# Turning x by DMA transposes of its half words in place of TensorE, in FFN pairs 1 and 3 and attention's first two blocks

## The reference

```
x = x + 0.5 * FFN(layernorm(x))
x = x + attention(layernorm(x))      # one head of 128, two sequences of 1024 rows
x = x + 0.5 * FFN(layernorm(x))
FFN(y) = (silu(y @ Wg) * (y @ Wu)) @ Wd     # Wg, Wu 512 x 1376, Wd 1376 x 512, 4-bit packed
```

## Time and profile before

| | us |
|---|---|
| median of 3 runs | 831.31 (831.05 to 831.92) |
| span of the profiled execution, first to last instruction | 829.4 |
| TensorE busy in it | 814.2 |
| VectorE, ScalarE, GpSimd busy | 494.9, 273.1, 252.1 |

### The profile page before, as it was taken

One profiled execution on the slowest core, in us unless ns is written; L12 is line 12 of the kernel. 1 busy time (PEld: TensorE's weight loads), 2 busy tenths in 40 slices (PEclk: granted clock), 3 DMA queues, 4 the chain that ended last, 5 costly groups with the idle time before them and its releaser, 6 DMA issues.

```text
span 829.4 us, 10560 instructions
## 1 busy us (share of the span) xinstructions
PE 814.2 (98%) x3932; PEld 670.7 (81%) x3932; DVE 494.9 (60%) x809; ACT 273.1 (33%) x471; POOL 252.1 (30%) x203
## 2 busy tenths in 40 slices
PE   4999999999999999999999999999999999999998
PEld 4777778878888888788898888888878888888786
DVE  7989945766554544547766896545346644443452
ACT  3433433555111121333656871111123311211221
POOL 5656614652115061303064371062401110110100
PEclk9999999999999999999999999999999999999999
DMA  6899958865854532234053159544454155344121
GB/s 164 275 331 295 326 185 298 342 243 210 287 181 140 175 130 71 105 108 152 1 178 128 40 183 379 198 154 151 127 166 142 49 194 175 128 154 150 30 102 51
DMA packets 73405, 143.04 MB, mean 172 GB/s; under 512 B 26092, under 2 KB 37028, under 8 KB 68362
## 3 DMA queue, kind: packets, MB, share of 16 engines
q1 hardware_dynamic: 66676, 130.97, 46.0%
q10 hardware_dynamic: 5814, 7.17, 2.5%
q0 software_dynamic: 864, 4.23, 1.9%
HBM read 104.30 MB, written 37.98 MB: 172 GB/s over the span
## 4 chain that ended last, share of the span: by engine, by line
PE 94%; POOL 1%; DVE 1%; DMA 1%; ACT 1%; issue 1%; ACTq 0%; SPq 0%; DVEq 0%; POOLq 0%
PE ps L813 53%; PE ps L806 37%; PE ps L824 2%; PE ps L1198 2%; DMA tab_rest<-sc_part 1%; POOL blk L2214 1%; PE ps L892 0%; ACTq L1538 0%; POOL xres L2324 0%; DMA zq_gu<-in_L_ffn_up_qzeros 0%; DVE stats L1718 0%; POOL xres L2329 0%; ACT xT L1315 0%; PE ps L1123 0%; POOL rstd L2219 0%
## 5 line engine op out<-in xcount | busy, mean ns | idle before, releaser
L806 PE MATMUL ps<-blk,ring 128*128 128x512 f32 (+1 forms) x1386 | 320.9, 389 | 0.5 <-POOL blk L2214 0.5
L806 PEld LDWEIGHTS ps<-blk,ring 128*128 128x128 f32 (+1 forms) x1386 | 256.7, 185 | 58.5 <-POOL blk L2214 1.0
L813 PE MATMUL ps<-wd,hT 128*128 128x512 f32 (+1 forms) x1056 | 251.6, 391 | 0.1
L813 PEld LDWEIGHTS ps<-wd,hT 128*128 128x128 f32 (+1 forms) x1056 | 197.0, 188 | 42.2 <-DVE h L1877 0.5
L2266 POOL TENSOR_TENSOR h<-h,u 128x512 f32<-128x512 f32 (+1 forms) x33 | 42.8, 1297 | 321.3 <-ACT h L1446 321.3
L813 PE MATMUL ps<-xT,wp 128*128 128x512 f32 x480 | 112.6, 390 | 0.3 <-issue 0.3
L813 PEld LDWEIGHTS ps<-xT,wp 128*128 128x128 f32 x480 | 89.8, 188 | 19.6 <-POOL wp L2214 0.6
L1710 DVE TENSOR_TENSOR u<-ps,p1s 128x512 f32<-128x512 f32 (+1 forms) x66 | 45.4, 688 | 95.8 <-PE ps L806 95.8
L1446 ACT ACTIVATE h<-h 128x512 f32<-128x512 f32 (+1 forms) x33 | 20.9, 632 | 177.4 <-DVE h L1710 177.4
L1710 DVE TENSOR_TENSOR h<-ps,p1s 128x512 f32<-128x512 f32 (+1 forms) x33 | 22.8, 691 | 63.9 <-PE ps L806 63.9
L1710 DVE TENSOR_TENSOR u<-ps,u 128x512 f32<-128x512 f32 (+1 forms) x66 | 45.6, 691 | 24.6 <-PE ps L806 23.5
(11 more groups left out here) (130 smaller groups left out, 894.5 us busy)
## 6 DMA issues: line engine op xcount, KB each, us to landing
ring<-wsaved SPq DMA_DIRECT2D x29, 1024.0 KB, 5.1
ring<-wsaved SPq DMA_DIRECT2D x33, 768.0 KB, 4.3
wsaved<-wp SPq DMA_DIRECT2D x10, 1024.0 KB, 5.0
stream<-xres SPq DMA_DIRECT2D x32, 256.0 KB, 2.4
xn<-stream SPq DMA_DIRECT2D x8, 1024.0 KB, 8.1
xres<-stream SPq DMA_DIRECT2D x32, 256.0 KB, 4.0
wfull<-wf ACTq DMA_DIRECT2D x20, 256.0 KB
wsaved<-wp SPq DMA_DIRECT2D x10, 512.0 KB, 5.5
```

What stands on the lines that cost most here:

```text
L806: mm = pe.matmul(ps[0:w, bank, :], ring[:, slot, which, a, kt, 0:w], blk[:, which, b, kt, :], start=not onto and kt == 0 and n == 0, stop= ...
L813: mm = pe.matmul(bank_ap, lhs(a), rhs(b), start=first and n == 0, stop=last and n == 2)
```

## The change

The three pieces of TensorE work in `bottom` are gone (96 transposes: blocks 2, 3, 4, 5, 10, 11). In their place, for each of these blocks: ScalarE copies each normalised tile of 128 rows into two planes of 16-bit words, the low and the high halves of its float32 values (`to_planes`, four copies of 128 x 1024 words a block, each waiting for the one before, since a tile's planes are written over the tile before it); SP stores the planes to DRAM (four DMAs of 256 KB) and issues one DMA transpose that reads the 1024 x 512 words of 16 bit and writes them turned into `xn`, where pairs of words form float32 values again. ScalarE and VectorE then read the turned tiles from SBUF, not from PSUM; the copy `x21` of A21 falls away in pairs 1 and 3.

```diff
+PLANED = (2, 3, 4, 5, 10, 11)
+        planes_early = place("planes_early", [P, 2, HID], U16, xres_at)
+        planes_late = place("planes_late", [P, 2, HID], U16, t13_at)
...
+            def store_planes(t):
+                for r in range(RT):
+                    sp.wait_ge(s_planes, planes_made(t, r))
+                    sp.dma_start(planes[t][r * P:(r + 1) * P, :, :], plane_rows(t, r)).then_inc(d_planes[t % 2], 16)
+
+            def turn_planes(t):
+
+                sp.wait_ge(*planes_stored(t))
+                sp.dma_start_transpose(xn[:, t % 2, :, :].bitcast(U16), planes[t].rearrange("n h c -> (n h) c")).then_inc(d_xT[t % 2], 16)
...
             store_rows(0, stream, 0)
-            load_residual(1, x, ROWS)
             for j in range(1, NT):
                 if j + 2 < NT:
                     load_full(j + 2)
                 save_t(j)
+                if j == 6:
+                    store_planes(2)
+                if j == 7:
+                    turn_planes(2)
+            store_planes(3)
 
             sp.wait_ge(s_up, 2 * NT)
             for i in (NT - 4, NT - 3, NT - 2, NT - 1):
                 sp.wait_ge(d_kept[i], ALL_KEPT)
             load_block(0)
+            turn_planes(3)
+            load_residual(1, x, ROWS)
             load_block(1)
...
                 load_block(n + 2)
+                if n in (6, 8):
+                    store_planes(4 if n == 6 else 5)
+                if n == 7:
+                    turn_planes(4)
+            turn_planes(5)
...
+                    if n in (NT + 6, NT + 9):
+                        store_planes(10 if n == NT + 6 else 11)
+                    if n in (NT + 7, NT + 10):
+                        turn_planes(10 if n == NT + 7 else 11)
...
-                    if i == first:
-
-                        pe.wait_ge(s_sum, 2 * RT * q + RT)
-                        if q == 1:
-                            pe.wait_ge(s_ln[4], RT)
-                            turn(4, range(KT))
-                        else:
-                            turn_pair(q + 1, 0)
-                    if i == second:
-                        if q == 1:
-                            pe.wait_ge(s_ln[5], RT)
-                            pe.wait_ge(s_alo, KT)
-                            turn(5, range(KT))
-                        else:
-                            turn_pair(q + 1, 1)
...
+            def to_planes(t, tiles=range(RT)):
+
+                for r in tiles:
+                    if r == 0:
+
+                        if t == 2:
+                            act.wait_ge(d_st[0], 16)
+                        elif t != 4:
+                            act.wait_ge(*planes_stored(PLANED[PLANED.index(t) - 1]))
+                    else:
+
+                        act.wait_ge(s_planes, planes_made(t, r - 1))
+                    act.wait_ge(s_ln[t], r + 1)
+                    copy(plane_rows(t, r), xn[:, t % 2, r, :].bitcast(U16).rearrange("p (c h) -> p h c", h=2)).then_inc(s_planes, 1)
...
                     if i in (5, 6, 8, 9):
                         ln_apply(2 if i < 7 else 3, (0, 1) if i in (5, 8) else (2, 3))
+                        to_planes(2 if i < 7 else 3, (0, 1) if i in (5, 8) else (2, 3))
...
             def pair(q, first=0):
+                t = {1: 4, 2: 10}.get(q)
                 for i in range(first, NT):
                     n = ordinal(q, i)
+                    if t and i in (5, 8):
+                        to_planes(t + (i == 8))
                     first_out(n)
                     silu_top(n)
...
             def tiles_hi(q, kt):
-                x21(q, kt)
                 x_hi(q, A11, kt)
...
                 def turned_tile(which):
 
+                    if q != 2:
+                        dve.wait_ge(*planes_turned(block_rows(q, which)))
+                        return turned_block(q, which, kt)
                     dve.wait_ge(s_xhi, split(q, which, kt))
```

More of the change, by code:

```diff
@@ L11 @@
 I32 = mybir.dt.int32
+U16 = mybir.dt.uint16
 ALU = mybir.AluOpType
@@ L265, in down_bank, with turn_at @@
             return 4 - LOW[q] + r if half == 0 else LOW[q] + (r - 1) % 4
[L267 to L271, removed]
+        def turn_at(what, kt):
+            return {A21: 4, A22: 6, A11: 6, A12: 6}[what] + kt
         TURN_BANK = (2, 3, 0, 1)
@@ L283, in macaron @@
         wfull = nc.dram_tensor("wfull", [NT, P, 2, HID], F32, kind="Internal").ap()
+        planes = {t: nc.dram_tensor(f"planes{t}", [ROWS, 2, HID], U16, kind="Internal").ap() for t in PLANED}
         stream = nc.dram_tensor("stream", [2 * TOKENS, HID], F32, kind="Internal").ap()
@@ L302, in macaron @@
         d_x0 = [sem(f"d_x0{n}") for n in range(RT)]
-        d_row = [None] + [sem(f"d_row{t}") for t in range(1, 12)]
+        d_row = [sem(f"d_row{n}") for n in range(2)]
         d_res = [sem(f"d_res{n}") for n in range(RT)]
+        d_planes = [sem(f"d_planes{n}") for n in range(2)]
+        d_xT = [sem(f"d_xT{n}") for n in range(2)]
         d_st = [sem(f"d_st{n}") for n in range(RT)]
@@ L342, in hidden, with turned, copied, block_rows @@
             return h2_back[:, NT - 1 - i, :]
[L345 to L346 removed]
+        ROWS_TURNED = 4 * KT
+        def turned(what, kt):
+            return ROWS_TURNED + TURN_HALVES.index((what, kt)) + 1
         def split(q, what, kt):
             return 6 * (q - 1) + (SPLIT_TILES if q % 2 else SPLIT_HALVES).index((what, kt)) + 1
[L351 to L353 removed]
+        def copied(kt, what=A21):
+            return kt + 1 + (2 if what == A11 else 0)
+        def block_rows(q, what):
+            return {1: 2, 3: 10}[q] + (what in (A21, A22))
+        def turned_block(q, what, kt):
+            return turned_rows(block_rows(q, what), kt + (2 if what in (A12, A22) else 0))
         def heads_split(a, j):
@@ L716, in _ @@
                 if n == 0:
-                    sp.wait_ge(s_turn, turned(1, A12, 1))
+                    sp.wait_ge(s_xlo, split(1, A12, 1))
                     stored(0)
@@ L787, in _ @@
                     if n == NT:
-                        sp.wait_ge(s_turn, turned(2, A12, 1))
+                        sp.wait_ge(s_turn, turned(A12, 1))
                         stored(6)
@@ L1224, in turn_ahead @@
                 for kt in range(2):
-                    turn_block(2, what, kt)
+                    turn_block(what, kt)
             def later_heads():
@@ L1402, in plain_bottom, with x21 @@
                 t_blocks_hi(NT - 1)
-            def x21(q, kt):
-                act.wait_ge(s_turn, turned(q, A21, kt))
-                copy(blk_f[:, S3, 1, kt, :], ps[:, turn_at(q, A21, kt), :]).then_inc(s_x21, 1)
+            def x21(kt):
+                act.wait_ge(s_turn, turned(A21, kt))
+                copy(blk_f[:, S3, 1, kt, :], ps[:, turn_at(A21, kt), :]).then_inc(s_x21, 1)
             def x11(kt):
-                copy(blk_f[:, S2, 1, kt, :], ps[:, turn_at(2, A11, kt), :]).then_inc(s_x21, 1)
+                copy(blk_f[:, S2, 1, kt, :], ps[:, turn_at(A11, kt), :]).then_inc(s_x21, 1)
             def x_hi(q, what, kt):
-                act.wait_ge(s_turn, turned(q, what, kt))
-                copy(blk[:, what, 0, kt, :], ps[:, turn_at(q, what, kt), :]).then_inc(s_xhi, 1)
+                if q == 2:
+                    act.wait_ge(s_turn, turned(what, kt))
+                    src = ps[:, turn_at(what, kt), :]
+                else:
+                    act.wait_ge(*planes_turned(block_rows(q, what)))
+                    src = turned_block(q, what, kt)
+                copy(blk[:, what, 0, kt, :], src).then_inc(s_xhi, 1)
             def sum_hi(q, what, kt):
@@ L1501, in bottom @@
                                     act.wait_ge(d_kept[tile], ALL_KEPT)
+                            elif q and kt == 0:
+                                act.wait_ge(s_P3, NT * q)
                             tiles_hi(q + 1, kt)
@@ L1611, in later_heads @@
                 for kt in range(2):
-                    x21(2, kt)
+                    x21(kt)
                     x_hi(2, A22, kt)
@@ L1988, in bottom @@
                         if i == at_ + 2:
+                            if q == 0 and kt == 0:
+                                for tile in range(NT - 4):
+                                    dve.wait_ge(d_kept[tile], ALL_KEPT)
+                            elif q and kt == 0:
+                                dve.wait_ge(s_P3, NT * q)
                             x_sum(q + 1, S1, kt)
```

86 lines of the change are left out of this document (46 added, 40 removed).

## The result

The changed kernel takes 855.32 us (854.58 to 858.07, 4 runs) against 831.24 (831.05 to 831.92, 4 runs): the ratio is 1.0292, with an interval of 1.0276 to 1.0308. It is slower by 24.1 us where 11.2 were forecast. The profiled execution has a span of 852.7 us, 23.3 more than before; it is the fastest of the four runs of the changed kernel, which lie 3.5 us apart.

The account below looks back on a forecast made before the run. TensorE, busy 98% of the span, was taken to bound the kernel. 13.6 + 4.55 - 3.5 - 3.5 = + 11.15 us gave a span of 840.6, so 842.5 us by the median; range 833 to 864.

Parts of the forecast that it names:

- both waits: TensorE waits ahead of P2 in pair(1) and pair(2), and in bottom(0) ahead of down 7 and 8.
- The step that failed: In pair(1) and pair(2), four ScalarE copies ahead of first_out delay P2 by 3.4 us, four times: 13.6 us.
- The second term: bottom(0): block 3 arrives late through DRAM, so the stage costs T - 3.55 us, + 4.55 us.
- T: Time from issue to landing of block 3's DMA transpose ahead of pair(1): 8.1 us, bounds 4.3 and 16.2.
- That VectorE and ScalarE read from SBUF in place of PSUM costs nothing I can see: Reading the turned tiles from SBUF adds no cost: ScalarE copies 630 ns against 580 to 600, low parts off the path.
- The transposes taken away: TensorE's transposes removed from the three bottom stages: 3.5 us saved a stage, 10.5 us in all.
- The DMA transpose: As a rival: a slow transposing DMA decides both bottom(0) and bottom(2); 854.6 us with T = 16.2; chance 0.21.
- that rival: The transposing DMA is slow in bottom(0) and bottom(2): T = 16.2 gives + 23.3, 854.6 us; chance 0.21.
- The estimate of 42 us: Block transpose by DMA as 32 tiles of 1309 ns one after another, giving a time of some 906 us.
- A copy's price: A ScalarE plane copy of 1024 words takes 1.07 us, plus 0.05 for waiting on the last: 1.12 us.
- What would show it: Signs: four TensorE idles of 3.4 us ahead of P2, waits ahead of down 7 and 8, pair(1) at about 214.7.
- the rival with quick copies: ScalarE's copies in the pairs take 0.35 us or less, off the path: 820.8 us; chance 0.08.

Follow-up runs that it names:

- Experiment 1: The changed kernel with ScalarE's to_planes moved from ahead of first_out to behind silu_top in pair(1) and pair(2): 833.88 us, 1.0028 of the kernel before.
- experiment 3: The changed kernel with 14 small identity products on TensorE ahead of P2's wait at i = 5 and 8 of pair(1) and pair(2): 847.49 us.
- experiment 11: Experiment 1 plus a wait in pairs 1 and 3: GpSimd's low parts start only after VectorE's low part of A22; 833.83 us.
- experiment 9: Experiment 1 plus block 3's planes stored behind save_t(8) and turned behind save_t(9): 825.99 us, 0.9931 of the kernel before.
- experiment 12: Experiment 9 and experiment 11 in one kernel: 825.05 us, 0.9920 of the kernel before.
- experiment 5: The changed kernel with turn_planes(3) issued ahead of load_block(0) in place of behind it: 851.94 us.

## Why the prediction was wrong

The direction and both waits were right, each at its place; the size was not: + 24.1 us against + 11.15, though 855.3 lies inside the range.

- **The step that failed** is the price of the wait ahead of P2, "P2 starts 3.4 us late ... 4 x 3.4 = 13.6 us". That number itself is right: four times 3.46 us from start to start are 13.8. What the sum lacks is what TensorE does behind them, a term put at nothing without a reason. The two pairs lose 21.2 us in the trace: 13.8 by the waits, 6.5 by slower products behind them (1.7, 1.7, 0.1 and 3.0), and 0.9 at the start of `pair(1)`. Experiment 1 gives 19.4 to 21.4 us back, and experiment 3 puts 6 to 8 of these on the granted clock. The kernel before had a clock of 1.00 in every stage read, and I took the product's 1.36 us from it as if it held behind a wait as well.
- **The second term**, `bottom(0)`, was T - 3.55 = + 4.55 us and was + 8.6, of which 0.9 stood there at 31 us already, and the rest is the term's: + 7.7. T was 9.3 us, not 8.1: 1.2 us. The issue at 193.0 and not 192.0 is the late start, so the time of the issue was forecast well, but not for the reason given: `load_block(0)` went 0.7 us sooner than forecast, and then SP waited 1.6 us for the stored planes. Another 1.7 us lie between the landing and hidden tile 8, and 1.4 of them are "That VectorE and ScalarE read from SBUF in place of PSUM costs nothing I can see". ScalarE's copies are the same (616 and 612 ns), but two of VectorE's differences took 2.36 us in place of 1.28 beside GpSimd, which experiment 11 shows, and the low part of hidden tile 8 took 1.08 in place of 0.77. The same thing stood in the kernel before, as the rows under this list show. The Trainium skill, "SBUF — State Buffer", section on the two separate sides, says that a VectorE operation with two SBUF inputs and a GpSimd operation that reads SBUF exclude one another; these rows agree.
- **The transposes taken away** were worth 3.5 us a stage: - 3.75 with attention, - 2.8 in `bottom(2)`, where 0.33 us of waits and the same slower differences stand.
- **The DMA transpose** was no rival after all. It moved at 290 GB/s when it was alone, 1 MB in 3.6 us, and landed 6.3 us after the issue at best, 10.5 at worst. With T of 9.3 us it never came near the 16.2 of that rival; that the rival's 854.6 us stand next to the measured time is chance, since the loss lay elsewhere. The estimate of 42 us worked out from the Trainium skill, "VectorE: DVE Perf Modes", section on the three transpose paths, with its 1309 ns tile after tile, is refuted. The 261 GB/s of the Trainium skill, "DMA: Bandwidth & Descriptors", section on latency and other measured facts, hold there for a non-contiguous middle dimension, which the prediction left out, and a contiguous transpose has some 350 to 400. The planes are read as one contiguous range, and the 290 measured lie above the one and below the other.
- **A copy's price** came out at the measured 1.04 to 1.08 us by a reading that is wrong in part: 382 ns for 256 elements and 630 for 512 make 0.97 ns for each element more, not "between 0.85 and 0.95", and by it 1024 elements would take 1.13 us. The 0.05 us for the wait of each copy for the last are not in the trace either, where `first_out` starts 4.2 us behind the first copy and not 4.4.
- **What would show it** held for the waits, the copies' duration and their order; the `pair(1)` start of 214.7 was 218.8. None of the signs by which the forecast was to be known as wrong appeared (waits under 2 us, a landing within 5 or after more than 12, idle time under 10 us): they looked at the waits only, and not at the products behind them. The change does what it says, and the rival with quick copies has nothing for it.

VectorE of the kernel before, in `bottom(0)`: two low parts with one operand in PSUM, beside GpSimd; two whose operands both lie in SBUF, without GpSimd beside them and with it. Then GpSimd's rows at the first time and the third.

```profile
195.00 1.28 DVE L1707 TENSOR_TENSOR blk<-ps,blk 128x512 fp32r<-128x512 f32 x2
...
198.79 1.28 DVE L1707 TENSOR_TENSOR blk<-blk_f,blk 128x512 fp32r<-128x512 f32 x2
...
207.25 2.39 DVE L1707 TENSOR_TENSOR blk<-blk_f,blk 128x512 fp32r<-128x512 f32 x2
...
194.63 1.61 POOL L2214 TENSOR_TENSOR blk<-blk_f,blk 128x512 fp32r<-128x512 f32 x1 [9.68 <-ACT blk L1315]
...
206.87 1.62 POOL L2214 TENSOR_TENSOR blk<-blk_f,blk 128x512 fp32r<-128x512 f32 x1 [0.78 <-DVE blk_f L1707]
```

## What to carry to other kernels

On an engine that runs its list in order, a piece of work costs nothing or all of itself by where it stands: look for the idle row that is long enough (5.57 us here, four copies of 1.08) and not for a low busy share. A wait put on a TensorE that was never idle has to be priced with the products behind it at half clock as well: where the list of waits says 3.3 us, each cost 5.1 us here on the mean (3.6 at the least, 6.4 at the most). And when tiles move from PSUM to SBUF, ask what GpSimd does beside VectorE at that moment.

## What the runs showed of the hardware

- Behind waits of 3.3 us the granted clock was at half speed for a while three times of four; behind four waits of 1.1 us and one of 1.76 us the products showed no fall, and behind one of 2.15 us and one of 2.18 us it fell. The first row is the 4.2 us behind the wait of 2.15 us in experiment 9: 11 products, at a granted clock of 0.59; the second the time from 0.8 us behind the wait of 1.76 us in experiment 12 (columns as in the earlier trace rows).

```profile
201.80:206.00 4.20, 4.17 (x11) 3.35 (x12) 4.11 (x7) 3.11 (x6) 0.28 (x1) 0.59 1.05 416
...
201.00:206.00 5.00, 5.00 (x23) 4.11 (x22) 4.91 (x9) 1.87 (x3) 0.16 (x1) 1.00 1.05 419
```

- A DMA transpose of 1 MB of 16-bit words keeps SP for 4.2 to 7.1 us, 2.9 us less for block 3 when the ring loads ahead of it are gone (experiment 5); the longest plain DMA issue of the changed kernel takes 2.1 us. Its rate and its issues in the changed kernel: one microsecond of the block 3 transfer (columns as in the earlier trace rows), and SP's quickest issue; the slowest is the 7.14 us of block 3, shown above.

```profile
200.00:201.00 1.00, 0.00 (x0) 0.00 (x0) 0.00 (x0) 0.00 (x0) 0.00 (x0) 1.00 1.27 290
```

```profile
345.30 4.20 SPq L636 DMA_TRANSPOSE xn<-planes  x1
```

- Copies that separate the halves of 32-bit words on ScalarE, with a stride of two words on the reading side, take 1.04 to 1.08 us for 1024 words. The float32 copies of 256 and 512 elements (382 and 630 ns) continued to 1024 would be 1.13 us by an estimate: no penalty for stride or for 16 bit shows, and no gain to speak of.
